# Attention scores laid out with queries on partitions: row maximum as a bias of the exponential, weights turned by transfers or TensorE

## The chip, the cores and the metric

One core of a Trainium2 chip runs the whole program. The core has TensorE (PE), VectorE (DVE), ScalarE (ACT), GpSimd (POOL) and SyncE (SP), which here only issues transfers. The metric is the time of one execution on the device, in microseconds (us); less is better.

## What is computed

The block is `x + attention(layernorm(x)) + ffn(layernorm(x))`, with x of 2 x 1024 tokens x 256. The change touches the attention alone, cut to its core:

```python
q = concat([q_nope, rope(q_rope)])      # 16 heads, 128 + 64 wide
k = concat([k_nope, rope(k_rope)])      # 4 heads, each shared by 4 query heads
attn = einsum('bhqd,bhkd->bhqk', q, k) * scale
attn = where(causal, -inf, attn)        # key > query
attn = softmax(attn, axis=-1)           # minus the row's maximum, exp, over its sum
out  = einsum('bhqk,bhkd->bhqd', attn, vh)
return out.reshape(B, T, H * 128) @ W_o
```

The feed-forward part is an integer-quantised pair of products (1024 inner columns); the change doesn't touch what it computes.

## The kernel before

**Steps.** The attention is a loop of 32 steps n: 4 key heads g, times 8 steps s (2 batches b, 4 query heads r each). A step handles one query head of one batch: 1024 queries by 1024 keys, the lower triangle. Rank 64 latent values stand for keys and values, so that a query or key vector is 128 long (64 latent and 64 rotated), and a value is 64 columns and one of ones (VC = 65), which gives the sum of the weights. Queries, keys and weights are split in a high and a low part, so a product takes three passes: high by high, high by low, low by high.

**Layout of a step.** Scores stand with keys on partitions: j is a tile of 128 keys, and its queries run along the row. `score_chunks` cuts the triangle in 12 chunks of 256 to 512 columns, 4,736 columns in all, into three PSUM banks (`score`, SBANKS = 3). Because the maximum of a query is then a maximum over partitions, the kernel takes it ahead: one to two steps before, `max_unit` forms high by high scores with queries on partitions (4,736 columns again, in `pmax`, two banks), `maxima` (line 863) lets VectorE take each row's maximum with the causal mask, TensorE turns the 8 columns of maxima (L1234), `cast_maxima` (L870, L872) makes two bf16 rows, and SyncE copies them to `m_row`. In `scores`, a product of `ones_b` with `m_row` subtracts the maximum: a fourth pass over each chunk. The names of matmuls in the rows are all at line 1078, the helper `mm`, so they are told apart by their tiles: `m_row,ones_b` is the row of maxima, `k_hi,q_hi` the pass for the maximum, `q_hi,k_hi`, `q_hi,k_lo`, `q_lo,k_hi` the three passes of a score, `kv_tok,p_hi` and `kv_tok,p_lo` the product with the values.

**After the scores.** ScalarE takes the exponential twice, once rounded to f16 (`p_hi`, L684) and once in place (L685); VectorE subtracts (`p_lo`, L996). Both parts are in the layout in which TensorE takes them as weights, and `values` accumulates 36 blocks of 128 x 128, three matmuls each, into the two `head` banks, two key tiles behind the scores.

**Queries.** Three steps ahead TensorE forms the queries of a step (`query`, slots 5 and 6), ScalarE copies them to `q_raw` (L613), GpSimd rotates them in four operations (`rotate`, L469, L472, L475, L478), ScalarE rounds them (`q_hi`, L617, a ring of three), and GpSimd subtracts (`q_lo`, L484).

**Order.** It is written out by hand. A step has 8 slots, one for each key tile; `MISC` and `EXTRA` give the slot of all that shares the one bank `misc`: queries, the turning of normalised heads (`turn`), the output product (`out`), keys of the next head (`ka`, `kb`), the integers of the feed-forward part (`w`, `x`). Each use of the bank waits until the one before is read (`misc_used`). Engines talk by semaphores; every engine works off its own list in order.

## Time and profile before

| | |
|---|---|
| time, median of 3 runs | 780.97 us (780.57 to 782.66) |
| the profiled execution | 779.53 us, of which 777.7 us are its span |
| TensorE busy | 729.5 us (94% of the span) |
| VectorE, ScalarE, GpSimd busy | 580.6, 496.3, 420.4 us |
| first and last pass `q_lo,k_hi` of a score | about 95.8 and 721.9 us after the start |
| four steps in the middle, from 418.3 us on | 18.1, 22.8, 18.2, 17.2 us |

A busy time on TensorE covers each matmul from its start to its modelled end, and matmuls overlap: what one costs in a full stream is the distance to the start of the next. The clock that TensorE was granted stands in the page in tenths, and for a stretch in the windows view, where 1.00 is 2.4 GHz and 0.50 is 1.2 GHz.

### The profile page before, as it was taken

The numbers are of one execution on the slowest core, as the hardware profiler recorded it, in microseconds if no ns is written. First come the engines' busy times: TensorE is split into PE (matmuls) and PEld (weight loads), VectorE is DVE, ScalarE is ACT, GpSimd is POOL, SyncE is SP. The second block draws the span as 40 slices with busy tenths as digits, with TensorE's granted clock in tenths as the row PEclk, the third lists the DMA queues.
The fourth block names the chain that finished last, engine by engine and source line by source line (L and its number), as shares of the span: only waits on it lengthen the run. The fifth ranks groups of instructions, "written<-read, shape, count | busy, mean of one in ns | idle before, by whom it ended". The sixth has DMA issues, their size and how long they took to land.

```text
span 777.7 us, 18089 instructions
## 1 busy us (share of the span) xinstructions
PE 729.5 (94%) x7010; PEld 582.9 (75%) x7084; DVE 580.6 (75%) x1530; ACT 496.3 (64%) x1015; POOL 420.4 (54%) x210
## 2 busy tenths in 40 slices
PE   7996699899999999999999999999999999999856
PEld 5664468688876678878877888788878888887635
DVE  6748478887777777777777768776777787776796
ACT  3555467577556565767577657765776577657754
POOL 4323546666655554676467646764676467620225
PEclk9786699999999999999999999999999999999989
DMA  9754002001300200010001000100000000000003
GB/s 261 256 201 178 1 1 82 16 15 42 124 1 29 82 28 2 21 43 23 2 1 30 1 15 16 42 15 2 1 29 2 1 2 2 2 1 3 14 0 109
DMA packets 20517, 33.08 MB, mean 43 GB/s; under 512 B 2704, under 2 KB 11472, under 8 KB 20304
## 3 DMA queue, kind: packets, MB, share of 16 engines
q1 hardware_dynamic: 19648, 31.34, 12.8%
q8 instruction: 56, 0.92, 0.5%
q10 hardware_dynamic: 784, 0.59, 0.3%
q14 instruction: 29, 0.24, 0.1%
HBM read 21.30 MB, written 10.49 MB: 41 GB/s over the span
## 4 chain that ended last, share of the span: by engine, by line
PE 78%; DVE 10%; issue 4%; ACT 4%; DMA 2%; POOL 1%; SPq 0%; POOLq 0%; ACTq 0%; DVEq 0%
PE psum L1078 74%; PE psum L1275 2%; DMA acc<-in_L_attn_x 2%; DVE hid L1058 1%; DVE small L1027 1%; ACT psum L685 1%; DVE p_lo L996 1%; POOL res L521 1%; ACT p_hi L684 1%; DVE acc L755 1%; PE psum L1101 1%; ACT hid L711 0%; PE psum L1326 0%; DVE kt_a L960 0%; PE psum L1234 0%
## 5 line engine op out<-in xcount | busy, mean ns | idle before, releaser
L684 ACT ACTIVATE p_hi<-psum 128x512 f16<-128x512 f32 (+3 forms) x384 | 187.7, 489 | 169.8 <-PE psum L1078 164.6
L996 DVE TENSOR_TENSOR p_lo<-psum,p_hi 128x512 f16<-128x512 f32 (+3 forms) x384 | 208.4, 553 | 85.7 <-ACT psum L685 84.5
L863 DVE CUSTOM_DVE_ANT_0 junk<-psum,cmask 128x1024 bf16<-128x1024 f32 (+7 forms) x256 | 187.8, 752 | 58.9 <-issue 57.4
L469 POOL TENSOR_TENSOR q_swap<-q_raw,sin_sb 32x1024 f32<-32x1024 f32 x31 | 73.6, 2374 | 228.9 <-ACT q_raw L613 220.5
L685 ACT ACTIVATE psum<-psum 128x512 f32<-128x512 f32 (+3 forms) x384 | 187.2, 487 | 0.0
L1078 PE MATMUL psum<-q_hi,k_hi 128*128 128x512 f32 (+2 forms) x384 | 187.0, 487 | 0.0
L1078 PEld LDWEIGHTS psum<-kv_tok,p_hi 128*128 128x128 f16 x2304 | 116.9, 97 | 53.4 <-issue 38.6
L1078 PE MATMUL psum<-kv_tok,p_hi 128*128 128x65 f16 (+1 forms) x2304 | 151.9, 196 | 0.4 <-DVE p_lo L996 0.4
L1078 PE MATMUL psum<-kv_tok,p_lo 128*128 128x65 f16 x1152 | 138.1, 192 | 0.0
L1078 PE MATMUL psum<-q_hi,k_lo 128*128 128x512 f32 (+2 forms) x384 | 132.1, 344 | 0.0
L1078 PE MATMUL psum<-q_lo,k_hi 128*128 128x512 f32 (+2 forms) x384 | 131.9, 343 | 0.0
L1078 PE MATMUL psum<-k_hi,q_hi 128*128 128x512 f32 (+3 forms) x384 | 106.0, 358 | 11.7 <-DVE small L863 7.7
L1078 PEld LDWEIGHTS psum<-kv_tok,p_lo 128*128 128x128 f16 x1152 | 109.0, 100 | 0.0
L1078 PE MATMUL psum<-m_row,ones_b 128*128 128x384 bf16 (+2 forms) x313 | 100.8, 322 | 1.4 <-DVE p_lo L996 1.4
L1078 PEld LDWEIGHTS psum<-k_hi,q_hi 128*128 128x128 f32 x384 | 65.5, 192 | 32.2 <-DVE small L863 21.3
L484 POOL TENSOR_TENSOR q_lo<-q_raw,q_hi 128x1024 fp32r<-128x1024 f32 x32 | 76.8, 2401 | 15.9 <-PE psum L1078 10.8
L1078 PEld LDWEIGHTS psum<-q_lo,k_hi 128*128 128x128 f32 x384 | 72.7, 189 | 7.3
L1078 PEld LDWEIGHTS psum<-q_hi,k_lo 128*128 128x128 f32 x384 | 73.8, 192 | 4.3
L472 POOL TENSOR_TENSOR q_swap<-q_raw,sin_sb 32x1024 f32<-32x1024 f32 x31 | 74.0, 2388 | 2.4
L475 POOL TENSOR_TENSOR q_raw<-q_raw,cos_sb 64x1024 f32<-64x1024 f32 x31 | 73.9, 2382 | 2.4
L478 POOL TENSOR_TENSOR q_raw<-q_raw,q_swap 64x1024 f32<-64x1024 f32 x31 | 73.6, 2375 | 2.4
L1078 PEld LDWEIGHTS psum<-q_hi,k_hi 128*128 128x128 f32 x384 | 73.9, 193 | 0.0
(172 smaller groups left out, 1205.8 us busy)
## 6 DMA issues: line engine op xcount, KB each, us to landing
wq_split<-w_split SPq DMA_DIRECT2D x4, 1024.0 KB, 5.5
k_rotated<-k_split SPq DMA_DIRECT2D x8, 512.0 KB, 3.7
wq<-wq_split SPq DMA_DIRECT2D x16, 256.0 KB, 2.7
acc<-in_L_attn_x SPq DMA_DIRECT2D x4, 512.0 KB, 7.7
ffn_t<-in_L_attn_W_o SPq DMA_DIRECT2D x1, 2048.0 KB, 20.7
k_hi<-k_rotated SPq DMA_DIRECT2D x8, 256.0 KB, 4.0
k_lo<-k_rotated SPq DMA_DIRECT2D x8, 256.0 KB, 4.5
w_split<-in_L_ffn_w SPq DMA_DIRECT2D x2, 1024.0 KB, 6.0
```

The source lines that it names most:

```text
L469: pool.tensor_tensor(q_swap[0:HR, :], raw[HR:ROPE, :], sin_sb[HR:ROPE, :], ALU.mult)\
L472: pool.tensor_tensor(q_swap[HR:ROPE, :], raw[0:HR, :], sin_sb[0:HR, :], ALU.mult)\
L475: pool.tensor_tensor(raw[0:ROPE, :], raw[0:ROPE, :], cos_sb[0:ROPE, :], ALU.mult)\
L478: pool.tensor_tensor(raw[0:ROPE, :], raw[0:ROPE, :], q_swap[:, :], ALU.add).then_inc(S["pool_step"], 1)
L484: pool.tensor_tensor(q_lo[s % 2][:, :], q_raw[s % 2][:, :], q_hi[n % QRING][:, :], ALU.subtract)\
L521: pool.tensor_tensor(y[:, :, :], y[:, :, :], acc[:, t:t + 2, :], ALU.add).then_inc(S["f_res"], 1)
L684: act.activation(p_hi[j % PRING][:, o:o + used], src, ACT.Exp, scale=SCALE)
L685: act.activation(src, src, ACT.Exp, scale=SCALE).then_inc(S["exp_done"], 1)
L863: ins = dve.tensor_tensor_reduce(junk[:, o:o + w], pmax[:, o:o + w], cmask[:, T - w:T], 1.0, LOWEST, ALU.add, ALU.max, mcol[:, s % 2, i:i ...
L996: dve.tensor_tensor(p_lo[j % PRING][:, o:o + used], score[c % SBANKS][:, w - used:w], p_hi[j % PRING][:, o:o + used], ALU.subtract).then_i ...
L1078: ins = pe.matmul(dst, lhs, rhs, start=start, stop=stop, skip_group_check=True)
L1275: ins = pe.transpose(misc[:, i * P:(i + 1) * P], o_norm[:, 4 * k + i, :], identf[:, :])
```

## The change

Scores now stand with queries on partitions. A step goes over 8 query tiles i in 7 units, in the order 7, 3, 6, 2, 5, (1, 0), 4: the *big* tiles 7, 6, 5, 4 take turns in two places of two PSUM banks each, the *small* ones 3, 2, 1, 0 share one bank.

- The score needs no pass for the maximum. VectorE takes the maximum straight from the scores, negated (`maxima`, L876), and ScalarE adds it as the exponential's bias. The pass of `m_row`, the pass ahead of `max_unit`, `cast_maxima` and the two small transfers of each step are gone. The scale goes into the copy of the queries.
- ScalarE takes each big tile in one operation of 640 to 1024 columns, twice (L676 and the next); a small tile once, in f32, to `p_f32`.
- VectorE subtracts for the big tiles from PSUM (`big_low`, L884, 3,328 columns in 4 operations). For all small tiles together, at the end of a step, it casts 1,280 columns of `p_f32` to f16 (L892) and subtracts (L894), both from SBUF to SBUF (`small_halves`).
- The weights have keys along the row and must be turned. Big tiles: SyncE issues 8 transposing transfers a step, `turn_big`, two for each tile (52 blocks of 128 x 128 in f16, 1.7 MB). Small tiles: in the next step TensorE turns 20 blocks through the bank `misc` in three turns of 8, 8 and 4 (L1283), and ScalarE copies each turn out (L689).
- `values` of tiles 6, 5, 4 and of the small ones come one step later, that of tile 7 at the end of its own step.
- Queries are formed two steps ahead, not three (`q_hi` is a ring of two); GpSimd rotates for the next step.
- `MISC` and `EXTRA` are laid out again over 7 slots.

The diff, cut to its core:

```diff
-CHUNKS = score_chunks()
-MAX_UNITS = [[(7, 0)], [(6, 0)], [(5, 0)], [(4, 0)], [(3, 0), (2, CH)], [(1, 0), (0, CH)]]
+UNITS = ((7,), (3,), (6,), (2,), (5,), (1, 0), (4,))
+BIG = {7: 0, 6: 1, 5: 2, 4: 3}
+SMALL = {3: 0, 2: 1, 0: 2}
+PSRC = 3
+COLS = {7: 0, 5: 0, 6: 2 * CH, 4: 2 * CH + P, 3: 4 * CH, 2: 4 * CH, 1: 4 * CH, 0: 4 * CH + 2 * P}
+PV_AT = {0: (6, 1), 2: (5, 1), 3: (4, 1), 6: (7, 0)}
+PV_SMALL = 4
...
+            def turn_big(n, i, h):
+                q, src = NB * n + BIG[i], slice(0, (i + 1) * P)
+                if n:
+                    sp.wait_ge(S["pv_done"], PV_STEP * (n - 1) + PV_DONE[i])
+                sp.wait_ge(S["lo_done" if h else "hi_done"], q + 1)
+                sp.dma_start(pt_big[i][:, h * (i + 1):(h + 1) * (i + 1), :], p_src[q % PSRC][:, h, src], transpose=True)\
+                  .then_inc(p_in[q % PSRC], 16)
...
-            rotate(2, 2, 6)
             for n in range(LAST):
+                if n + 1 < LAST:
+                    rotate(n + 1, n + 1, misc_index(n - 1, "query", 1) + 1 if n else 4)
...
-                if n + 3 < LAST:
-                    rotate(n + 3, n + 3, misc_index(n, "query", 1) + 1)
-                if n + 2 < LAST:
-                    pool.wait_ge(S["score_done"], NC * (n + 1))
-                    query_low(n + 2, n + 2)
+                if n + 1 < LAST:
+                    query_low(n + 1, n + 1)
...
-                            act.activation(p_hi[j % PRING][:, o:o + used], src, ACT.Exp, scale=SCALE)
-                            act.activation(src, src, ACT.Exp, scale=SCALE).then_inc(S["exp_done"], 1)
+                        act.activation(p_src[q % PSRC][:, 0, 0:w], src, ACT.Exp, bias=nb).then_inc(S["hi_done"], 1)
+                        act.activation(src, src, ACT.Exp, bias=nb).then_inc(S["exp_done"], 1)
+                    else:
+                        if n:
+                            act.wait_ge(S["small_lo"], n)
+                        ins = act.activation(p_f32[:, OFF[i]:OFF[i] + w], src, ACT.Exp, bias=nb)
...
+            def maxima(n, u):
+                dve.wait_ge(S["score_done"], NS * n + u + 1)
+                for i in UNITS[u]:
+                    dve.tensor_reduce(sm["mcol"][:, NT * (n % 2) + i:NT * (n % 2) + i + 1],
+                                      psum[:, COLS[i]:COLS[i] + (i + 1) * P], AX.X, ALU.max, negate=True)\
+                       .then_inc(S["max_done"], 1)
...
+            def small_halves(n):
+                dve.wait_ge(S["small_free"], len(SMALL) * (n + 1))
+                if n:
+                    dve.wait_ge(S["misc_full"], misc_index(n, "pt", 2) + 1)
+                dve.tensor_copy(p_small[:, 0, :], p_f32[:, :]).then_inc(S["small_hi"], 1)
+                dve.wait_ge(S["small_hi"], n + 1)
+                dve.tensor_tensor(p_small[:, 1, :], p_f32[:, :], p_small[:, 0, :], ALU.subtract).then_inc(S["small_lo"], 1)
...
-                mm(o, ones_b[:, 0:P], m_row[s % 2][:, qs], not diagonal, False)
-                mm(o, k_hi[b][:, ks], qh[:, qs], False, False)
-                mm(o, k_lo[b][:, ks], qh[:, qs], False, False)
-                mm(o, k_hi[b][:, ks], ql[:, qs], False, True, S["score_done"])
+                        mm(o, qh[:, qs], k_hi[b][:, ks], not diagonal, False)
+                        mm(o, qh[:, qs], k_lo[b][:, ks], False, False)
+                        ins = mm(o, ql[:, qs], k_hi[b][:, ks], False, True)
...
+            def turn_small(m, k, idx):
+                pe.wait_ge(S["small_lo"], m + 1)
+                pe.wait_ge(S["misc_used"], idx)
+                for t, (h, i, j) in enumerate(TURNS_B[k]):
+                    o = OFF[i] + j * P
+                    ins = pe.transpose(misc.bitcast(F16)[:, t * P:(t + 1) * P], p_small[:, h, o:o + P], ident16[:, :])
+                ins.then_inc(S["misc_full"], 1)
```

Three places show what the order has become. On VectorE, at the end of a step and the beginning of the next, before (the maxima of later steps between the subtractions of this one):

```order
L996 TENSOR_TENSOR p_lo0<-psum,p_hi0 128x512 [waits pv_done,exp_done]
L996 TENSOR_TENSOR p_lo0<-psum,p_hi0 128x512 [waits exp_done]
L860 MEMSET small 128x1 [waits max_done]
L863 ISA junk,small<-psum,cmask 128x640
L863 ISA small 128x1
L996 TENSOR_TENSOR p_lo1<-psum,p_hi1 128x512 [waits pv_done,exp_done]
L888 RECIPROCAL small<-psum 128x4 [waits pv_done]
L892 TENSOR_TENSOR o_norm<-psum,small 128x4x64 [waits norm_step]
```

and now (the last two operations of a step are L892 and L894; the row behind them is the maximum of the next step's tile 7):

```order
L884 TENSOR_TENSOR p_src1<-psum,p_src1 128x768 [waits exp_done]
L876 TENSOR_REDUCE small<-psum 128x1 [waits score_done]
L911 TENSOR_TENSOR o_lo1<-psum,o_hi1 128x512 [waits o_hi_done]
L892 CAST p_small<-p_f32 128x1280 [waits misc_full,small_free]
L894 TENSOR_TENSOR p_small<-p_f32,p_small 128x1280 [waits small_hi]
L876 TENSOR_REDUCE small<-psum 128x1 [waits score_done]
L884 TENSOR_TENSOR p_src2<-psum,p_src2 128x640 [waits exp_done]
L876 TENSOR_REDUCE small<-psum 128x1 [waits score_done] x2
L884 TENSOR_TENSOR p_src0<-psum,p_src0 128x1024 [waits exp_done]
```

Every maximum now stands between the scores of its own tile and that tile's exponential, and the two operations on the small tiles come behind the maximum of tile 4, the last of the step. On TensorE, in the first slots of a step, before:

```order
L1078 MATMUL psum<-k_hi1,q_hi0 128x512 [waits max_read]
L1078 MATMUL psum<-k_hi1,q_hi0 128x256
L1078 MATMUL psum<-m_row0,ones_b 128x512 [waits lo_done]
L1078 MATMUL psum<-q_hi2,k_hi1 128x512
L1078 MATMUL psum<-q_hi2,k_lo1 128x512
L1078 MATMUL psum<-q_lo0,k_hi1 128x512
L1078 MATMUL psum<-kv_tok,p_hi2 128x65 [waits lo_done]
```

and now, behind the scores of tile 7 and the values of tile 6 (the last row is that of those values):

```order
L1084 MATMUL psum<-kv_tok,pt_big6 128x65
L1283 MATMUL psum<-ident16,p_small 128x128 [waits misc_used,small_lo]
L1283 MATMUL psum<-ident16,p_small 128x128 x7
L1084 MATMUL psum<-cmask,ident 128x128 [waits small_free]
L1084 MATMUL psum<-k_hi0,q_hi1 128x512
L1084 MATMUL psum<-k_lo0,q_hi1 128x512
L1084 MATMUL psum<-k_hi0,q_lo1 128x512
L1283 MATMUL psum<-ident16,p_small 128x128 [waits misc_used,small_lo]
L1283 MATMUL psum<-ident16,p_small 128x128 x7
L1084 MATMUL psum<-k_hi0,q_hi1 128x512 [waits lo_done]
```

The passes with `m_row` and with `max_read` are gone, and the turns of the small tiles stand there, the first behind `small_lo`, which L894 gives. On GpSimd a step is these five rows in either kernel; now:

```order
L468 TENSOR_TENSOR q_swap<-q_raw1,sin_sb 32x1024 [waits misc_used,qlo_done]
L471 TENSOR_TENSOR q_swap<-q_raw1,sin_sb 32x1024 [waits pool_step]
L474 TENSOR_TENSOR q_raw1<-q_raw1,cos_sb 64x1024 [waits pool_step]
L477 TENSOR_TENSOR q_raw1<-q_raw1,q_swap 64x1024 [waits pool_step]
L483 TENSOR_TENSOR q_lo1<-q_raw1,q_hi1 128x1024 [waits pool_step,qhi_done]
```

The first waits for the second half of the queries, which now leaves `misc` in slot 5 of 7 of a step; the fifth no longer waits for `score_done`.

## Rows read from the trace of the kernel before

**Rows 1.** The page: busy time by engine, and TensorE's granted clock in tenths

```profile
PE 729.5 (94%) x7010; PEld 582.9 (75%) x7084; DVE 580.6 (75%) x1530; ACT 496.3 (64%) x1015; POOL 420.4 (54%) x210
PEclk9786699999999999999999999999999999999989
```

**Rows 2.** Windows of four steps, 418.3 to 494.6 us: their sums and means

```profile
sum 76.30, PE 76.30 PEld 62.85 DVE 57.94 ACT 51.42 POOL 47.56; mean PE 19.07 PEld 15.71 DVE 14.49 ACT 12.85 POOL 11.89
```

**Rows 3.** The page: the chain that ended last, share by engine

```profile
PE 78%; DVE 10%; issue 4%; ACT 4%; DMA 2%; POOL 1%; SPq 0%; POOLq 0%; ACTq 0%; DVEq 0%
```

**Rows 4.** Timeline of PE at 404 us: start, duration, line, tiles, size

```profile
404.08 0.39 PE L1078 MATMUL psum<-qc_lo,wq 128*128 128x512 f32 x1
404.31 0.39 PE L1078 MATMUL psum<-qc_hi,wq 128*128 128x512 f32 x1
```

**Rows 5.** Timeline of PE, 145.9 to 149.1 us; in brackets the idle time ahead

```profile
145.90 0.22 PE L1078 MATMUL psum<-kv_tok,p_hi 128*128 128x65 f16 x2
...
145.99 0.22 PE L1078 MATMUL psum<-ident,cmask 128*128 128x128 bf16 x1
146.04 0.33 PE L1078 MATMUL psum<-m_row,ones_b 128*128 128x384 bf16 x1
146.07 0.47 PE L1078 MATMUL psum<-q_hi,k_hi 128*128 128x384 f32 x1
146.38 0.33 PE L1078 MATMUL psum<-q_hi,k_lo 128*128 128x384 f32 x1
146.55 0.34 PE L1078 MATMUL psum<-q_lo,k_hi 128*128 128x384 f32 x1
149.00 0.51 PE L1078 MATMUL psum<-k_hi,q_hi 128*128 128x256 f32 x2 [2.11 <-DVE small L863]
```

**Rows 6.** Groups of instructions by form: count, busy us, mean ns, idle before

```profile
L996 DVE TENSOR_TENSOR p_lo<-psum,p_hi 128x512 f16<-128x512 f32 x160 | 110.2, 689 | 65.4 <-ACT psum L685 65.4
L996 DVE TENSOR_TENSOR p_lo<-psum,p_hi 128x384 f16<-128x384 f32 x96 | 53.1, 553 | 17.7 <-ACT psum L685 16.9 <-DVE m_cast L872 0.4
L1027 DVE TENSOR_REDUCE small<-hid 128x1 f32<-128x1024 f32 x16 | 18.7, 1213 | 2.5 <-ACT hid L711 2.5
L684 ACT ACTIVATE p_hi<-psum 128x512 f16<-128x512 f32 x160 | 95.4, 596 | 120.3 <-PE psum L1078 118.6
L631 ACT ACTIVATE ffn_t<-psum 128x1024 bf16<-128x1024 bf16 x2 | 2.1, 1030 | 0.0
```

**Rows 7.** Timeline of DVE's operations from SBUF to SBUF, and POOL's beside them

```profile
144.99 2.86 DVE L966 TENSOR_SCALAR acc<-acc,small 128x1024 f32<-128x1024 f32 x1
144.94 2.36 POOL L478 TENSOR_TENSOR q_raw<-q_raw,q_swap 64x1024 f32<-64x1024 f32 x1
147.53 2.53 POOL L484 TENSOR_TENSOR q_lo<-q_raw,q_hi 128x1024 fp32r<-128x1024 f32 x1 [0.24 <-POOL q_raw L478]
152.98 0.74 DVE L966 TENSOR_SCALAR acc<-acc,small 128x1024 f32<-128x1024 f32 x1
231.72 0.97 DVE L960 TENSOR_TENSOR kt_a<-kt_a,kt_b 128x512 f32<-128x512 f32 x1
229.75 2.38 POOL L478 TENSOR_TENSOR q_raw<-q_raw,q_swap 64x1024 f32<-64x1024 f32 x1
259.87 0.69 DVE L960 TENSOR_TENSOR kt_a<-kt_a,kt_b 128x512 f32<-128x512 f32 x1
```

**Rows 8.** Windows around the wait at 146.9 us: busy time, then granted clock (PEclk)

```profile
146.80:150.20 3.40, 1.29 (x16) 1.01 (x15) 3.40 (x9) 0.87 (x2) 3.03 (x2) 1.00 0.00 0
150.30:153.60 3.30, 2.98 (x20) 2.61 (x21) 2.76 (x10) 1.25 (x3) 0.00 (x0) 0.50 0.02 5
```

**Rows 9.** Transfers: count, KB each, us from issue to landing; SP's own time

```profile
k_rotated<-k_split SPq DMA_DIRECT2D x8, 512.0 KB, 3.7
wq<-wq_split SPq DMA_DIRECT2D x16, 256.0 KB, 2.7
k_lo<-k_rotated SPq DMA_DIRECT2D x8, 256.0 KB, 4.5
L368 SPq DMA_DIRECT2D m_row<-m_cast x64: 620/633/1130, 90.8 to 707.4; - x64
```

575 lines of the change are left out of this document (265 added, 310 removed).

## The prediction

> **What bounds the kernel now.** I read the page first: TensorE is busy for 94% of the span, and its clock stands at the full level from the fourth slice nearly to the end [rows 1]. The chain of work that ended last is TensorE's for 78%, with no other engine over 10% [rows 3]. The windows of four steps settle it: 76.3 us, in all of which TensorE is busy, while VectorE has 14.49 us of work in a mean step of 19.07, ScalarE 12.85 and GpSimd 11.89 [rows 2]. So a step costs what TensorE's stream costs, and nothing waits. The question for the change is how much it takes out of that stream, and whether the stream stays unbroken.
>
> **What leaves and enters TensorE's stream.** A matmul costs the distance to the start of the next. A pass over 512 columns costs 0.23 us [rows 4], so the pass for the maximum, 4,736 columns, costs 4,736 / 512 x 0.23 = 2.1 us a step. For the row of maxima, `m_row` and the first pass of a 384-column chunk take from 146.04 to 146.38, 0.34 us together, and the next pass alone 0.17 [rows 5]; so the row costs 0.17 for 384 columns, 2.1 us for 4,736. Removed: 4.2 us. Added: 20 turns of 128 x 128 in f16, at the price of the 128-wide bf16 matmul ahead of `m_row`, 0.05 us (145.99 to 146.04) [rows 5]: 1.1 us with their weight loads. The three passes of a score and the 36 blocks of values (0.09 us each, 145.90 to 145.99 [rows 5]) stay. TensorE's work falls by 3.1 us, from 19.07 to 16.0 us a step.
>
> **The other engines.** ScalarE: two widths, 596 ns for 512 columns and 1,030 for 1,024, give 0.85 ns a column and 0.16 us fixed [rows 6]. Twelve operations and 1,280 columns fewer save 3.0 us, and the copies of the turns (1.03, 1.03, 0.6) add 2.7: even, and far from a bound. VectorE: 689 and 553 ns for 512 and 384 columns give 1.06 ns a column and 0.15 fixed [rows 6]; eight subtractions and 1,280 columns fewer save 2.5 us, and the two operations on the small tiles add 2.4 (below). The maximum costs what a reduction of 1,024 columns does, 1.2 us, about as now. VectorE stays at some 14 us, under 16. GpSimd's five operations stay. None of these becomes the bound by its sum of work.
>
> **The new wait.** The bound comes from an order of events at each step's end. The last scores of a step are those of tile 4. Only then does VectorE take their maximum (640 columns, 0.82 us), and behind it, in its list, it casts the small tiles' 1,280 columns and subtracts. TensorE can't turn the small tiles before `small_lo`, and its own work in between is short: values of tile 7 (8 x 0.09 = 0.7), scores of tile 7 (six passes of 0.23 and a mask, 1.4), values of tile 6 (0.6), in all 2.8 us. Everything of the next step is queued behind this turn on TensorE, and on ScalarE the copy of the turn stands ahead of the exponentials of tile 7, so no engine can run past it.
>
> How long do the two operations take? The like of the cast, from SBUF to SBUF, took 0.74 us for 1,024 columns with GpSimd idle, and the like of the subtraction 0.69 for 512 [rows 7]. With 256 and 768 more columns (0.53 and 1.04 ns each) that is 0.88 and 1.49 us. But the same instructions took 2.86 and 0.97 us with GpSimd at work [rows 7]: the first started at 144.99, 0.05 us behind GpSimd's L478, and ended at 147.85, 0.55 us after L478's end at 147.30; the second started at 231.72 and ended 0.56 us after L478's end at 232.13. Both stood still until GpSimd's instruction was over, and GpSimd's next one, started at 147.53, took 2.53 in place of 2.38: it stood still for VectorE's rest. In the new order GpSimd is at work there for certain: the queries leave `misc` in slot 5 of 7, and from then on four operations of 2.38 us follow each other. The cast can wait for up to 2.38 us, and the subtraction, which has to wait for the cast, finds GpSimd's next operation in possession: up to 2.38 again. Bounds: 0 and 4.8 us. I take 3.0, the second wait nearly in full and the first in part (the cast may come first, where the queries were late).
>
> The Trainium skill (SBUF — State Buffer, Who interferes with whom) says the same more sharply: a cast in a two-port mode, or an operation with two SBUF inputs, and a GpSimd operation exclude each other for a whole instruction, and the one that issues second waits. By that rule alone, with both in full, the sum would hold 4.8 in place of 3.0 us, some 55 us more in all; by a mere sharing of bandwidth (0.97 to 0.69 as a ratio of 1.4) it would hold 1.0 in place of 3.0.
>
> Sum, from the end of the last scores: 0.8 (maximum) + 0.6 (what VectorE still has ahead of it: the subtraction of tile 5 or the low half of a turned head) + 0.9 + 1.5 + 0.1 (two semaphores) = 3.9; less 2.8 of cover, 1.1; plus 3.0 of standing still: TensorE waits **4.1 us a step**. Before, the list on TensorE had no wait for an operation of its own step's end.
>
> **Smaller waits.** The three turns share `misc`. The second must wait for ScalarE's copy of the first, 1.03 us and two semaphores, under a cover of 0.7 (scores of tile 3): 0.5. The third waits behind two exponentials of 1,024 columns (1 us each): 0.5. The small bank's next scores: 0.3. Turned heads now wait for a normalisation of the same slot, in two steps of four: 0.5 on average. Sum 1.8 us, between 0 and 3.
>
> **Transfers.** 1.7 MB a step are turned by 8 transfers. SyncE spends 0.63 us on a small one [rows 9], 5 us a step, within its time. Moving: no row shows a turning transfer. From 2.7 us for 256 KB to 3.7 for 512 KB [rows 9] is 1 us for 256 KB, 6.6 us a step. The latency, 2 to 4.5 us, has cover: a tile's values come four or five slots of some 3 us later. The upper bound takes each 256 KB as a transfer by itself, 4.5 us as `k_lo` [rows 9]: 6.5 x 4.5 = 29 us a step, more than a step has. I take the lower, as the transfers may overlap.
>
> The Trainium skill prices it twice: 261 GB/s for turning transfers (DMA: Bandwidth & Descriptors, Latency and other measured facts), by which a step's take 6.6 us, and 1,309 ns for a block of 128 x 128 (VectorE: DVE Perf Modes, The three transpose paths); as a rate that would be 52 x 1.3 = 68 us a step and a kernel of over 2,200 us.
>
> **The clock.** A wait of 2.11 us left 1.29 us of work in a window of 3.4 us [rows 5, 8]; in the next window the granted clock was 0.50, that is 1.2 GHz, and then it rose again. A wait of 4.1 us in each step should bring the same in each. At half the clock 3.4 us of stream lose 1.7 us; bounds 0 and 1.7 a step. I take 0.7, since part of that stretch waits for ScalarE anyhow.
>
> **Sum.** A step: 16.0 + 4.1 + 1.8 = 21.9 us, and 0.7 for the clock, 22.6, against 19.07: +3.5. For 31 steps with a step behind them that is +109. Ahead of the loop the passes for the first maxima and two small transfers fall away, behind it the last step's turns and values stand uncovered: some 10 us each, which I set against each other. 777.7 + 109 = 787 + 100, that is 887 us of span; with the 1.8 us around it 889, and the median stands 1.4 above the profiled execution: **about 888 us**.
>
> **Rivals.**
> 1. *GpSimd is out of the way*, so that the small tiles' operations need 2.4 us, and VectorE has nothing ahead of them. The wait falls to 0.5, a step to 16.0 + 0.5 + 1.8 = 18.3, the clock holds: 31 x -0.8 = -25, **about 756 us**. It decides from the length of the wait: with the smaller waits at 1.8, everything under 1.3 us is faster than before. For it speaks only that GpSimd works 11.89 of 19 us [rows 2]; against it, that these are the same microseconds. Its limit, no waits at all, is 31 x -3.1 = -96, 685 us. Chance 0.08.
> 2. *The transfers don't keep up.* At 29 us a step instead of 19: 31 x 10 = +310, **about 1,090 us**. TensorE would then wait for `p_in` and ScalarE for a free `p_src` (three buffers). Chance 0.09.
> 3. The forecast, new wait with GpSimd's part: 0.83. Its own range: half the blocking and no fall of the clock, 16.0 + 2.6 + 1.8 = 20.4, +41, 820 us; full blocking and 1.2 for the clock, 16.0 + 5.9 + 1.8 + 1.2 = 24.9, +180, 960 us.
>
> **Range and chances.** The forecast's own range, cut to 945 at the top, where full blocking in each of 31 steps is unlikely, and let down to 800 at the bottom for a blocking of a third, holds all but 2 in 10 of the chance: 800 to 945 us. This kernel's runs can tell a difference of about 0.3%. Faster: most of rival 1, 0.06. Same: 0.03. Slower: 0.91.
>
> **What the new profile would show.** The removal: TensorE's groups of `m_row` and of the pass for the maximum gone, its work without waits near 16 us a step. The wait: among the waits, TensorE's turns of `p_small` held by VectorE's L894, some 31 times, 3 to 5 us each. The blocking: L892 with a mean near 2 us and not 0.9, L894 near 3.5 and not 1.5, each ending a fixed time after an operation of GpSimd's. The clock: half the level behind each wait. The transfers: landing within 2 to 5 us, and nobody waiting for `p_in`. I am wrong in the mechanism if L892 and L894 together take under 3 us, and in the sign if TensorE's wait for them is under 1.3 us a step.

## The result, and the profile after

The changed kernel takes **930.73 us** (median of three runs, 925.66 to 933.94) against 780.97 before: a ratio of 1.190, 95% interval 1.181 to 1.199. The forecast was 888 us, range 800 to 945. The side, the mechanism and the range held; the time is 43 us over the forecast.

The page of the changed kernel, its busy times and the granted clock, and its chain by engine, answer [rows 1] and [rows 3]:

```profile
PE 732.6 (79%) x6919; PEld 570.3 (61%) x6922; DVE 651.1 (70%) x826; ACT 527.8 (57%) x727; POOL 462.7 (50%) x210
...
PEclk9666898899987898779989998988988998989898
...
PE 44%; DVE 30%; ACT 17%; issue 6%; DMA 2%; POOL 1%; POOLq 0%; ACTq 0%; SPq 0%
```

TensorE has gone from 94% of the span to 79%, and the chain that was TensorE's for 78% is now TensorE's for 44% and VectorE's for 30%. The clock, which before stood at 9 from the fourth slice on, dips all through the loop.

Four steps in the middle, from one cast of the queries to the fifth, answer [rows 2]. A row has start and end, length, then busy time and number of instructions of PE, PEld, DVE, ACT and POOL, and the granted clock:

```profile
515.67:538.05 22.38, 17.58 (x197) 14.11 (x195) 15.54 (x18) 14.35 (x22) 13.42 (x5) 0.92 0.44 75
538.05:562.80 24.75, 20.68 (x219) 17.22 (x218) 16.77 (x22) 13.27 (x20) 13.44 (x5) 0.93 0.39 77
562.80:588.36 25.56, 20.17 (x204) 16.03 (x203) 18.98 (x25) 14.43 (x21) 13.39 (x5) 0.87 0.39 78
588.36:608.63 20.27, 16.30 (x182) 12.61 (x181) 15.97 (x19) 13.03 (x19) 13.40 (x5) 0.92 0.64 120
sum 92.96, PE 74.73 PEld 59.97 DVE 67.27 ACT 55.07 POOL 53.65; mean PE 18.68 PEld 14.99 DVE 16.82 ACT 13.77 POOL 13.41
```

A mean step is 23.24 us long and holds 18.68 of TensorE's work; before, both were 19.07. So 4.6 us of each step are waits of TensorE.

Which waits, is in the list of waits (engine, its instruction, what released it: us in total, times, longest):

```profile
PE psum L1283 <- DVE p_small L894: 94.8, 32, 4.5
...
PE psum L1291 <- ACT q_raw L609: 17.4, 14, 1.9
...
PE psum L1084 <- ACT pt_small L689: 15.9, 17, 1.1
...
PE psum L1283 <- ACT pt_small L689: 5.0, 12, 1.2
```

The first is the wait of the prediction: the first turn of the small tiles behind VectorE's subtraction, 3.0 us a step on average, in every step. SBUF is the memory in which the program's own tiles lie (`p_f32`, `p_small`, `q_raw`), PSUM the one that the matmuls write. Why the subtraction comes so late is in the groups (count, busy us, mean ns), to be held against [rows 7]:

```profile
L894 DVE TENSOR_TENSOR p_small<-p_f,p_small 128x1280 f16<-128x1280 f32 x32 | 108.7, 3396 | 1.1
...
L474 POOL TENSOR_TENSOR q_raw<-q_raw,cos_sb 64x1024 f32<-64x1024 f32 x31 | 92.6, 2986 | 2.4
L471 POOL TENSOR_TENSOR q_swap<-q_raw,sin_sb 32x1024 f32<-32x1024 f32 x31 | 88.9, 2866 | 2.4
...
L892 DVE CAST p_small<-p_f 128x1280 f16<-128x1280 f32 x32 | 49.0, 1530 | 2.2 <-ACT p_f L681 2.2
```

and, for one step's end, in the timelines of VectorE, GpSimd and TensorE, one fence for each (start, duration):

```profile
543.80 0.94 DVE L892 CAST p_small<-p_f 128x1280 f16<-128x1280 f32 x1
544.77 3.52 DVE L894 TENSOR_TENSOR p_small<-p_f,p_small 128x1280 f16<-128x1280 f32 x1
```

```profile
541.66 2.39 POOL L468 TENSOR_TENSOR q_swap<-q_raw,sin_sb 32x1024 f32<-32x1024 f32 x1
544.13 2.81 POOL L471 TENSOR_TENSOR q_swap<-q_raw,sin_sb 32x1024 f32<-32x1024 f32 x1
547.02 3.49 POOL L474 TENSOR_TENSOR q_raw<-q_raw,cos_sb 64x1024 f32<-64x1024 f32 x1
```

```profile
544.51 0.82 PE L1084 MATMUL psum<-kv_tok,pt_big 128*128 128x65 f16 x21
548.35 0.62 PE L1283 MATMUL psum<-ident,p_small 128*128 128x128 f16 x8 [3.01 <-DVE p_small L894]
```

The subtraction started at 544.77, 0.64 us behind the start of GpSimd's L471. It ended at 548.29, 1.35 us after that operation's end at 546.94, and an undisturbed one takes 1.49 (below). So it stood still for about 2 us. The same distances, within 0.02 us, stand in the 30 steps in which GpSimd is at work there; in the last two steps, without it, the subtraction took 1.49. GpSimd pays as well: L471 began at 544.13, while the cast was still running (it ended at 544.74), and took 2.81 in place of 2.38; L474 began at 547.02, while the subtraction was running, and took 3.49.

The clock around the longest of the waits (4.5 us, 571.0 to 575.5) answers [rows 8]; after the bracketed counts stands the granted clock:

```profile
568.50:571.90 3.40, 2.42 (x28) 1.69 (x28) 3.38 (x3) 2.04 (x3) 3.24 (x3) 1.00 0.48 95
571.90:575.30 3.40, 0.00 (x0) 0.00 (x0) 3.39 (x1) 0.00 (x0) 3.32 (x2) 0.74 0.06 11
575.30:578.70 3.40, 3.21 (x21) 2.60 (x21) 2.64 (x4) 2.14 (x3) 2.34 (x1) 0.50 0.03 7
578.70:582.00 3.30, 3.30 (x34) 2.52 (x33) 0.99 (x2) 2.54 (x4) 0.00 (x0) 0.75 0.92 192
```

With the wait the clock falls to 0.50, and what follows (3.21 us busy of 3.40) runs at it. Over the whole span 245 us lie at half the clock, against 59 before.

The turning transfers, the answer to [rows 9]: SyncE's time for an issue (least, median, most, ns), and the median time to landing:

```profile
L369 SPq DMA_TRANSPOSE pt_big<-p_src x256: 1199/1232/3807, 91.8 to 868.3; - x128
```

```profile
pt_big<-p_src SPq DMA_TRANSPOSE x256, 3.1
```

TensorE waited for them three times, 2.8 us in all.

Outside of the steps: the first low by high pass of a score (`k_hi,q_lo`, before `q_lo,k_hi`) starts at 87.0 us (95.8 before), and behind the last one, at 862.1, there are 66.8 us (55.8 before): -9 and +11, which nearly cancel.

### The profile page after: what moved, and what is told of

Its sections match the earlier page's. It is cut to its first block, busy times and chain, and to the rows that moved or that the text cites. A ratio compares the mean times of both kernels' runs of the same rounds, so it can differ in the third digit from the quotient of the medians.

```text
span 928.9 us, 17035 instructions
## 1 busy us (share of the span) xinstructions
PE 732.6 (79%) x6919; PEld 570.3 (61%) x6922; DVE 651.1 (70%) x826; ACT 527.8 (57%) x727; POOL 462.7 (50%) x210
## 4 chain that ended last, share of the span: by engine, by line
PE 44%; DVE 30%; ACT 17%; issue 6%; DMA 2%; POOL 1%; POOLq 0%; ACTq 0%; SPq 0%
PE psum L1084 36%; DVE p_small L894 12%; PE psum L1283 6%; DVE p_small L892 5%; ACT p_src L676 4%; ACT pt_small L689 4%; DVE small L876 3%; ACT psum L677 3%; DVE p_src L884 3%; ACT q_raw L609 2%; DVE o_lo L911 1%; ACT q_hi L614 1%; DMA pt_big<-p_src 1%; PE psum L1291 1%; ACT o_hi L664 1%
## 5 line engine op out<-in xcount | busy, mean ns | idle before, releaser
L876 DVE TENSOR_REDUCE small<-psum 128x1 f32<-128x1024 f32 (+7 forms) x256 | 189.5, 751 | 117.8 <-PE psum L1084 117.6
L483 POOL TENSOR_TENSOR q_lo<-q_raw,q_hi 128x1024 fp32r<-128x1024 f32 x32 | 75.8, 2369 | 316.2 <-ACT q_hi L614 316.2
L689 ACT ACTIVATE pt_small<-psum 128x1024 f16<-128x1024 f16 (+1 forms) x96 | 84.9, 884 | 201.6 <-PE psum L1283 201.5
L1084 PE MATMUL psum<-k_hi,q_hi 128*128 128x512 f32 (+2 forms) x384 | 179.1, 466 | 24.9 <-POOL q_lo L483 13.5
L676 ACT ACTIVATE p_src<-psum,small 128x1024 f16<-128x1024 f32 (+3 forms) x128 | 121.8, 951 | 52.9 <-DVE small L876 51.1
L1283 PE MATMUL psum<-ident,p_small 128*128 128x128 f16 x640 | 71.8, 273 | 99.9 <-DVE p_small L894 94.8
L1084 PE MATMUL psum<-k_lo,q_hi 128*128 128x512 f32 (+2 forms) x384 | 145.6, 379 | 0.0
L1084 PE MATMUL psum<-k_hi,q_lo 128*128 128x512 f32 (+2 forms) x384 | 145.1, 378 | 0.0
L884 DVE TENSOR_TENSOR p_src<-psum,p_src 128x1024 f16<-128x1024 f32 (+3 forms) x128 | 129.9, 1014 | 15.5 <-ACT psum L677 15.2
L1283 PEld LDWEIGHTS psum<-ident,p_small 128*128 128x128 f16 x640 | 52.1, 124 | 119.8 <-DVE p_small L894 98.7
L677 ACT ACTIVATE psum<-psum,small 128x1024 f32<-128x1024 f32 (+3 forms) x128 | 118.5, 926 | 0.0
L894 DVE TENSOR_TENSOR p_small<-p_f,p_small 128x1280 f16<-128x1280 f32 x32 | 108.7, 3396 | 1.1
L1084 PE MATMUL psum<-kv_tok,pt_big 128*128 128x65 f16 (+1 forms) x2496 | 103.2, 197 | 2.8 <-DMA pt_big<-p_src 2.8
L1084 PEld LDWEIGHTS psum<-kv_tok,pt_big 128*128 128x128 f16 x2496 | 87.9, 100 | 25.1 <-issue 20.8
L474 POOL TENSOR_TENSOR q_raw<-q_raw,cos_sb 64x1024 f32<-64x1024 f32 x31 | 92.6, 2986 | 2.4
L471 POOL TENSOR_TENSOR q_swap<-q_raw,sin_sb 32x1024 f32<-32x1024 f32 x31 | 88.9, 2866 | 2.4
L477 POOL TENSOR_TENSOR q_raw<-q_raw,q_swap 64x1024 f32<-64x1024 f32 x31 | 82.0, 2646 | 2.4
```

The lines of the kernel that those rows point to most:

```text
L471: pool.tensor_tensor(q_swap[HR:ROPE, :], raw[0:HR, :], sin_sb[0:HR, :], ALU.mult)\
L474: pool.tensor_tensor(raw[0:ROPE, :], raw[0:ROPE, :], cos_sb[0:ROPE, :], ALU.mult)\
L477: pool.tensor_tensor(raw[0:ROPE, :], raw[0:ROPE, :], q_swap[:, :], ALU.add).then_inc(S["pool_step"], 1)
L676: act.activation(p_src[q % PSRC][:, 0, 0:w], src, ACT.Exp, bias=nb).then_inc(S["hi_done"], 1)
L677: act.activation(src, src, ACT.Exp, bias=nb).then_inc(S["exp_done"], 1)
L689: act.activation(pt_small[:, 8 * k:8 * k + m, :], misc.bitcast(F16)[:, 0:m * P].rearrange("p (t q) -> p t q", q=P), ACT.Copy)\
```

## The experiments

All are edits of the changed kernel. Each was timed beside the kernel before (780 to 782 us); ratios are to that.

**1. GpSimd out of the way.**

```diff
             for n in range(LAST):
+                if n:
+                    pool.wait_ge(S["small_lo"], n)
                 if n + 1 < LAST:
...
```

> Edit: GpSimd starts the rotation of the next step's queries only after VectorE has finished both operations on the small tiles of the step before; the two operations, their order and all of VectorE's other work stay. Theory A (GpSimd's operation stops VectorE's): in the changed kernel the cast took 1.53 us on average and the subtraction 3.40, and the last two steps, without GpSimd, showed 0.82 and 1.49. So they should fall to about 0.82 and 1.49, 2.6 us a step, TensorE's wait at the first turn from 3.0 to under 1 us a step; 31 x 2.6 = 80 us from 930.7 gives 850, and if the clock then stays up as well, down to 800. Theory B (the slow pair comes from the transposing transfers' use of SBUF, or is simply late in VectorE's list): the two operations stay near 1.5 and 3.4 us and the time near 925 to 935. Theory C (the wait moves to the low half of the queries, which GpSimd now makes later): the pair gets short, but TensorE waits for q_lo by some 2 us a step and the time stays over 880.

Measured: **825.5 us**, ratio 1.055 (1.052 to 1.058). The two groups, the mean of four steps, and the wait that is left:

```profile
L896 DVE TENSOR_TENSOR p_small<-p_f,p_small 128x1280 f16<-128x1280 f32 x32 | 47.8, 1492 | 1.1
L894 DVE CAST p_small<-p_f 128x1280 f16<-128x1280 f32 x32 | 35.6, 1111 | 1.3 <-ACT p_f L683 1.0
```

```profile
sum 80.23, PE 69.16 PEld 55.39 DVE 57.42 ACT 55.21 POOL 47.40; mean PE 17.29 PEld 13.85 DVE 14.36 ACT 13.80 POOL 11.85
```

```profile
PE psum L1285 <- DVE p_small L896: 23.6, 23, 1.2
```

Not one operation was taken away, and 105 us are gone. The subtraction is at 1.49 us in all 32 steps, the cast at 0.82 in 24 of them and near 2.0 in the other eight, mostly every fourth, where it meets GpSimd's low half of the queries (L483). Theory A holds: 825.5 lies between its 850, for the waits alone, and its 800, with the clock back up. The granted clock in these four steps is 1.00. A step went from 23.24 to 20.06: TensorE's busy time from 18.68 to 17.29 and its waits from 4.6 to 2.8, so that 1.4 of the 3.2 us came from the clock. At the first turn the wait fell by 2.3 us a step in these steps, from 3.1 to 0.8; TensorE's other waits rose by 0.5.

**2. No operation from SBUF to SBUF: the small tiles from PSUM.** ScalarE takes the exponential of a small tile twice; VectorE subtracts in three operations.

```diff
-                        ins = act.activation(p_f32[:, OFF[i]:OFF[i] + w], src, ACT.Exp, bias=nb)
+                        act.activation(p_small[n % 2][:, 0, OFF[i]:OFF[i] + w], src, ACT.Exp, bias=nb)
+                        ins = act.activation(src, src, ACT.Exp, bias=nb)
...
-                dve.tensor_copy(p_small[:, 0, :], p_f32[:, :]).then_inc(S["small_hi"], 1)
...
-                dve.tensor_tensor(p_small[:, 1, :], p_f32[:, :], p_small[:, 0, :], ALU.subtract).then_inc(S["small_lo"], 1)
...
+                dve.tensor_tensor(p_small[n % 2][:, 1, OFF[i]:OFF[i] + w], psum[:, COLS[i]:COLS[i] + w],
+                                  p_small[n % 2][:, 0, OFF[i]:OFF[i] + w], ALU.subtract).then_inc(S["small_lo"], 1)
```

> Edit: the two SBUF to SBUF operations are gone. ScalarE takes each small tile's exponential twice, as for the big tiles (high half in f16 to a ring of two, then in place), and VectorE subtracts for a small tile from PSUM, in three operations of 512, 384 and 384 columns spread over the step; the first turn needs the high halves alone. GpSimd's order is unchanged. Theory A (what costs is the pair of operations that GpSimd can stop, and its place behind the step's last maximum): TensorE's wait at the first turn, 3.0 us a step, nearly vanishes, VectorE's subtractions take 0.55 to 0.7 us as the like ones do; ScalarE gets 1280 columns and 4 operations more, 1.7 us a step, within its time. 31 x 3.0 = 93 us and the clock's share back: 790 to 840 us. Theory B (the extra time lies in transfers or in ScalarE's copies of the turns): little changes, or ScalarE's extra 1.7 us a step shows, 900 to 960.

Measured: **840.8 us**, ratio 1.075 (1.068 to 1.082). VectorE's group of 512 columns, GpSimd's L473, and what TensorE waits for now:

```profile
L473 POOL TENSOR_TENSOR q_raw<-q_raw,cos_sb 64x1024 f32<-64x1024 f32 x31 | 73.2, 2362 | 2.4
...
L889 DVE TENSOR_TENSOR p_small<-psum,p_small 128x512 f16<-128x512 f32 x32 | 22.0, 688 | 18.4 <-ACT psum L679 18.4
```

```profile
PE psum L1082 <- DVE p_small L889: 43.4, 41, 2.1
```

GpSimd works beside VectorE as in the changed kernel, and neither stops the other: a subtraction from PSUM takes 0.69 us, GpSimd's operations 2.36. TensorE no longer waits for VectorE at the turns. That is theory A, just past the slow end of its range (790 to 840). A new wait came in: the bank of the small tiles is free for the next scores only when VectorE has subtracted, 43.4 us in all. That this wait, and not ScalarE's further work, keeps the run at the slow end was not tried.

**3. The transfers left out.**

```diff
+                if n == 0:
                     sp.dma_start(pt_big[i][:, h * (i + 1):(h + 1) * (i + 1), :], p_src[q % PSRC][:, h, src], transpose=True)\
                       .then_inc(p_in[q % PSRC], 16)
+                else:
+                    sp.sem_inc(p_in[q % PSRC], 16)
```

> Edit: the transposing transfers are issued in step 0 alone; in all later steps SyncE only counts the semaphore up, so big tiles are multiplied with step 0's turned weights (the output is then not the block's; the transfers' moving is what is left out, all waits stay in place). Theory A (blocking by GpSimd, transfers hidden): TensorE waited for turned weights for 2.8 us in all, so the time falls by 0 to 10 us, 920 to 931, and the subtraction on the small tiles stays at 3.4 us. Theory B (the transfers cost: they slow SBUF accesses of VectorE and GpSimd, or hold a weights' buffer): the subtraction falls towards 1.5 us, GpSimd's operations from 2.6 to 3.0 us back to 2.4, and the time to 850 or less.

Measured: **928.6 us** (924.2 to 931.3), no difference from 930.7. The subtraction on the small tiles stays as it was:

```profile
L897 DVE TENSOR_TENSOR p_small<-p_f,p_small 128x1280 f16<-128x1280 f32 x32 | 108.7, 3398 | 1.1
```

1.7 MB of turning transfers a step cost nothing here, neither by waits nor by slowing another engine (GpSimd's four rotations take 2.49, 2.88, 3.01 and 2.62 us on average, and 2.49, 2.87, 2.99 and 2.65 with the transfers). Rival 2 is out.

**4 and 6. The clock alone: 14 and 24 filling products ahead of the wait.**

```diff
+                pe.wait_ge(S["misc_used"], idx)
+                if k == 0:
+                    keep_clock(misc, 14)
                 pe.wait_ge(S["small_lo"], m + 1)
-                pe.wait_ge(S["misc_used"], idx)
```

> Edit: ahead of its wait for the small tiles' low half TensorE does 14 bf16 products of 256 columns into the bank that it is about to write (at 0.11 us each about 1.5 us at full clock), which nobody reads; all else stays. It measures what the clock costs. Theory A1 (the idle of 3 to 4.5 us in each step lets the granted clock fall, and the fall costs time): the time at half the clock falls from 245 us to under 130, and the kernel from 930.7 to 870 to 900 us, since a stretch of 3.4 to 7 us at half the clock holds 2 to 4 us of work that would take half of that. Theory A2 (the fall lies where TensorE waits anyway): the time at half the clock falls but the kernel stays within 925 to 935. If the filling is too short for the clock, the stretches stay at 245 us and the run says nothing on the price; if it is too long, it delays the turn and adds up to 31 x 1.5 = 47 us.

> Edit: as in the run with 14 filling products, with 24 of them (2.6 us at full clock at 0.11 each). With 14 the time at half the clock fell from 245 to 139 us and the kernel from 930.7 to 908.0. Theory A1 (what the clock's fall costs is in proportion to the time at half the clock, 23 us for 105): with a clock that falls nearly only ahead of the loop and behind it, some 60 to 100 us at half, the price falls by another 10 to 15 us, less what the filling delays: where it outlasts the wait (1.8 us in the shortest steps, 3.3 to 4.4 in the others) 0 to 0.8 us in one step of four, 0 to 6 us in all: 893 to 905 us. Theory A2 (14 already took all there was to take): 908 to 925, since the filling delays the turns.

Measured: **908.0 us** with 14 (906.5 to 909.5) and **894.5** with 24 (894.0 to 904.5). The time at half the clock is 245 us without filling, 139 with 14, 70 with 24. The granted clock of both, 14 first:

```profile
PEclk7776999899997999699999999999999999999988
```

```profile
PEclk9667999999999999999999999999999999999988
```

Each microsecond less at half the clock gave back 0.21 us, both times (22.7 for 106, 36.2 for 175). The subtraction stays at 3.40 us in both. So of the changed kernel's loss some 36 to 39 us (the 186 us that it has more at half the clock, times 0.21) are the clock's, by an edit that leaves the late data where they were. It is rather more than that: with 24 the filling outlasts the subtraction by about 0.9 us in every fourth step, so that the edit costs something too.

**5. VectorE's order: the two operations ahead of the last maximum** (slot j = 6).

```diff
+                            small_halves(n)
                         maxima(n, j)
...
-                    if n < LAST and j == 6:
-                        small_halves(n)
```

> Edit: VectorE does the two operations on the small tiles ahead of the maximum of the step's last tile (4) and no longer behind it; GpSimd's order stays. It tests the term of the prediction that puts 0.8 us of the wait down to that maximum and 0.6 to what else stands ahead. Theory A (the operations are stopped by GpSimd wherever they stand): they still take 1.5 to 2 and 3.4 us, TensorE's first turn gets its data up to 0.8 us earlier, but the maximum, and with it the exponentials of tile 4, come 3 to 5 us later, so that the wait reappears at ScalarE and in TensorE's next big tiles: 925 to 950 us. Theory B (the place in VectorE's list is the cost): the wait of 3.0 us falls by 0.8 to 1.4, and 25 to 45 us go: 885 to 905.

Measured: **937.1 us** (935.2 to 938.3). The subtraction, ScalarE's wait for the maximum, and TensorE's waits at the turns:

```profile
L894 DVE TENSOR_TENSOR p_small<-p_f,p_small 128x1280 f16<-128x1280 f32 x32 | 109.2, 3413 | 1.1
```

```profile
ACT p_src L676 <- DVE small L876: 219.4, 65, 7.0
...
PE psum L1282 <- DVE o_lo L911: 58.4, 15, 4.6
...
PE psum L1282 <- DVE p_small L894: 15.8, 9, 1.8
...
PE psum L1282 <- DVE acc L917: 14.2, 7, 2.2
```

Theory A. GpSimd stops the two operations there as well, and another place in the list only makes something else late. TensorE's wait for the subtraction fell from 94.8 to 15.8 us, but at the same turns it now waits 58.4 and 14.2 us for L911 and L917, the two operations by which VectorE frees the shared bank and which stand behind the pair now: 88.4 us together, so that next to nothing was won there. ScalarE's wait for the maxima rose from 51 to 219 us.

**7. As 1, and the high halves by ScalarE**, so that VectorE's cast is gone.

```diff
+                        act.activation(p_small[:, 0, OFF[i]:OFF[i] + w], src, ACT.Exp, bias=nb)
                         ins = act.activation(p_f32[:, OFF[i]:OFF[i] + w], src, ACT.Exp, bias=nb)
...
-                dve.tensor_copy(p_small[:, 0, :], p_f32[:, :]).then_inc(S["small_hi"], 1)
...
-                pe.wait_ge(S["small_lo"], m + 1)
+                if k == 0:
+                    pe.wait_ge(S["small_free"], len(SMALL) * (m + 1))
+                else:
+                    pe.wait_ge(S["small_lo"], m + 1)
```

> Edit: GpSimd starts behind the small tiles' operation, as in the first experiment (825.5 us), and besides ScalarE writes the high halves of the small tiles itself (a second exponential of each, f16), so that VectorE's cast is gone, the first turn waits for no VectorE operation at the step's end, and the subtraction alone is left there. Theory A (what is left of the wait, 23.6 us at small_lo in that run, and its share of the clock, comes from the 0.82 us cast and the 1.49 us subtraction behind the last maximum): 825 less 15 to 25 gives 800 to 810 us. Theory B (ScalarE, 528 of 822 us busy, is by now what the turns wait for; 1.7 us a step more on it): the gain is eaten, 820 to 840, as in the run that took all small tiles from PSUM (840.8).

Measured: **807.8 us**, ratio 1.034 (1.029 to 1.039), theory A. ScalarE's 1.7 us more a step (578 us busy in all) cost less than the cast at the step's end had.

**8 to 11. A version that beats both.** High halves by ScalarE; low halves of tiles 3 and 2 from SBUF in mid-step, where GpSimd waits for the queries; those of tiles 1 and 0 from PSUM. Besides three placings: the queries' cast in slot 2, tile 6's values in slot 1, turns of 8, 7 and 5 blocks. In the diff `small_low` takes the step, its first tile, its blocks of 128 columns, its last tile, and whether the source is PSUM.

```diff
-PV_AT = {0: (6, 1), 2: (5, 1), 3: (4, 1), 6: (7, 0)}
+PV_AT = {1: (6, 1), 2: (5, 1), 3: (4, 1), 6: (7, 0)}
...
-QHI_SLOT = 4
+QHI_SLOT = 2
...
+                        if j == 3:
+                            small_low(n, 3, 4, 3, False)
+                        if j == 5:
+                            small_low(n, 2, 3, 2, False)
                         maxima(n, j)
...
+                        if j == 6:
+                            small_low(n, 1, 3, 0, True)
```

> Edit: the version that the traces point to. ScalarE writes the high halves of the small tiles; VectorE subtracts tile 3 and tile 2 from f32 in SBUF in the middle of the step (512 and 384 columns, ahead of the maxima of slots 3 and 5), when GpSimd in the changed kernel has nothing to do (it waited 316 us for the cast of the queries), and tiles 1 and 0 from PSUM, where GpSimd can't stop it, at the step's end. Besides: the cast of the queries in slot 2, the first two turns of the step further apart from the values (tile 6's values a slot later), turns of 8, 7 and 5 blocks. Theory A (with both causes of the wait gone, blocking and order, TensorE's stream of some 16 to 17 us a step shows): no wait for the small tiles over 0.5 us, a step of 18.0 to 19.0 us, 755 to 790 us in all. Theory B (the shared bank for turns, queries and heads, and ScalarE with 18 us of work a step, are the bound at 20 us): 800 to 825.

> Edit: of the best version (773.6 us) only what has nothing to do with the small tiles' halves: the cast of the queries in slot 2, tile 6's values in slot 1, turns of 8, 7 and 5 blocks. VectorE's cast and subtraction stay at the step's end. Theory A (the best version's gain comes from the halves made elsewhere and earlier): the subtraction stays near 3.4 us and TensorE's wait at 3 us a step or longer, since tile 6's values no longer stand between the first scores and the turn, so 0.6 us of cover is lost: 925 to 955 us. Theory B (the placing of the other work gives a good part of the gain by itself): 890 us or less.

> Edit: of the best version only the small tiles' halves: high halves by ScalarE; low halves of tiles 3 and 2 by VectorE from SBUF in mid-step, of tiles 1 and 0 from PSUM at the end. The queries' cast, the values and the turns stay as in the changed kernel. Theory A (the wait for the small tiles was the cost): 930.7 less 110 to 130 us; with what is left of ScalarE's copies and late queries, 800 to 820 us, better than the run that kept a subtraction from SBUF at the end (807.8) by 0 to 10, and the subtractions in mid-step mostly at 0.55 to 0.7 us. Theory B (ScalarE is the bound): as the run with all from PSUM, 835 to 845.

> Edit: the best version (773.6 us) with the turns of the small tiles put ahead of the values of the same slot in TensorE's list, the values of tiles 6, 5, 4 in slots 0, 1, 2 and those of the small ones in slot 3. What is left in its trace are waits of TensorE of 0.6 us for the small bank behind the last turn and of 0.8 to 1.2 for the shared bank, some 7 us in four steps. Theory A: the values now cover ScalarE's copies of the turns, 0.2 to 0.3 us a step, 763 to 772 us. Theory B (SyncE's transfers now come too late for values a slot earlier, or the stream is as full as it gets): 772 to 780.

Measured, in the order of the expectations: halves and placings together (8) **773.6 us** (ratio 0.990, 0.985 to 0.994); the placings alone (9) 944.5 (940.6 to 946.5); the halves alone (10) 808.4 (806.1 to 815.9); and (11) both with the turns ahead of the values and the values a slot earlier, **761.2 us**, ratio 0.975 (0.972 to 0.978).

Theory A holds in 8, 9 and 10; 11 came out 2 us under the range of its theory A. The placings alone cost 14 us: TensorE's wait for the subtraction grew to 138.8 us, as tile 6's values no longer covered it (first fence). The same placings on top of the new halves gave 35: TensorE's waits for ScalarE's copies of the turns, for the shared bank ahead of the turned heads and for the low half of the queries were 19.9, 17.8 and 12.9 us with the halves alone (second fence), and 5.9, 11.2 and none with both:

```profile
PE psum L1284 <- DVE p_small L895: 138.8, 32, 7.0
```

```profile
PE psum L1291 <- ACT pt_small L690: 19.9, 49, 2.4
...
PE psum L1299 <- ACT q_raw L609: 17.8, 14, 1.7
PE psum L1090 <- POOL q_lo L483: 12.9, 9, 1.9
```

A miss: with the halves alone I expected the subtractions in mid-step mostly undisturbed. That of tile 2 was (0.55 us), that of tile 3 took 0.89 on average instead of 0.68, since in 12 steps it met GpSimd's last rotation (L477). And the run was not faster than run 7. Mid-step is not free of GpSimd with the queries' cast in slot 2 either: in run 8 tile 2's subtraction took 0.94 us on average, since in half of the steps it met the low half of the queries (L484). The last version, its busy times, clock and four steps:

```profile
PE 665.0 (88%) x6922; PEld 521.3 (69%) x6922; DVE 554.0 (73%) x858; ACT 578.0 (76%) x855; POOL 417.6 (55%) x210
...
PEclk9786599999999999999999999999999999998989
```

```profile
sum 74.31, PE 68.75 PEld 55.36 DVE 54.52 ACT 61.55 POOL 47.55; mean PE 17.19 PEld 13.84 DVE 13.63 ACT 15.39 POOL 11.89
```

A step of 18.58 us with 17.19 of TensorE's work; 19.07 before. So scores with queries on partitions do pay, by 2.5%. Taking what GpSimd can stop from between the last scores and the first turn is needed for it and is not enough: by itself (runs 7 and 10) it left the kernel 3.4 and 3.8% slower than before, and only together with the placings is it faster. The last version's gain of 12 us over 773.6 lies mostly in the first half of the loop (10 us over its 16 steps), where keys and integers share the bank. Nearly 8 of them are shorter waits of TensorE for ScalarE's copies of the turns ahead of the keys' and integers' products (9.4 us in place of 17.1).

## Why the prediction was right, and where it was off

Steady steps first: forecast 22.6 us, measured 23.24 over four steps, each term against its own measurement. The terms as written add up to 890 us and not 888 (889 and 1.4), a slip that changes nothing.

- **TensorE's work: 16.0 forecast, 17.3 measured** (the granted clock at 1.00 in run 1; 17.2 in the last version). The step that failed here is the price of the row of maxima. I read 0.34 us for `m_row` and the first pass together [rows 5], took off 0.17, the price of the pass after, and put 2.1 us a step on `m_row`. Summing the distance from each matmul to the start of the next over the four steps of [rows 2] and over the four of run 1, the first pass of a chunk costs 0.25 us and the second 0.18 even without `m_row`: 0.07 of what I gave to the row belong to the first pass itself. Before, the mask, `m_row` and the first pass cost 4.65 us a step together; in run 1 the mask and the first pass cost 3.32. So the row was worth 1.3 us and not 2.1. The pass for the maximum was 2.3 (forecast 2.1), the turns 1.25 (forecast 1.1), and the values rose from 3.4 to 3.7, the queries from 2.4 to 2.5, the turned heads and the output product from 1.8 to 2.0, which I had left unchanged. Net -1.8, not -3.1.
- **The new wait: 4.1 forecast, 3.1 measured** in those steps (3.16, 3.01, 4.47 and 1.81), 3.0 over all; every fourth step it is 1.8 and not 3 to 5. The blocking was as said: L894 3.40 us (forecast 3.5) and L892 1.53 (forecast near 2), together 2.6 over what they take undisturbed (forecast 3.0). What was mis-sized is the cover. From the end of the last scores to the end of the subtraction the four steps took 7.3 us (forecast 6.9: the pair 5.0 and not 5.5, what stands ahead of it 2.3 and not 1.4). Of that time TensorE's other work and waits covered 4.2 us and not 2.8, with the clock up (run 1) as with it down. I had left out three things, one of which stands there in each of the four steps: the turned heads (0.8 us, twice), the output product (1.5) and a wait of 1.8 for GpSimd's low half of the queries, which is why the wait of that fourth step is the shortest. Both halves of the cause are shown: with GpSimd moved (run 1) or PSUM as source (run 2) it is gone; without the transfers (run 3) or in another order (run 5) it stays. The Trainium skill (SBUF — State Buffer, Who interferes with whom) has the rule: an operation with two SBUF inputs, or a cast in a two-port mode, and one of GpSimd's exclude each other; the trace agrees, with 4.93 us for the pair beside GpSimd's operations and 2.31 without.
- **Smaller waits: 1.8 forecast, 1.5 measured** (TensorE's idle time of 4.6 in the four steps less the 3.1). The sum held by luck. The second and third turn, forecast at 1.0, waited 0.2, and the small bank, forecast at 0.3, next to nothing; the turned heads waited 0.55 (forecast 0.5), but for ScalarE's copy of the queries and not for a normalisation; and 0.45 are that wait for the low half of the queries (1.8 in one step of four), for which the sum had no term.
- **The clock: 0.7 forecast, 1.3 to 1.4 measured**, by two roads: 18.68 of busy time against 17.29 with the clock at 1.00, and 0.21 x 186 / 31 = 1.3 from the filling runs. I had 0.7 for 3.4 us at half the clock, 0.21 a microsecond, and that price is the one that the filling runs gave. The length was short: 186 / 31 = 6.0 us of a step are at half the clock that were not before (in these four steps it is 4.3, at 0.33 of TensorE's busy time a microsecond).
- **Errors that cancel.** +1.3, -1.0, -0.3, +0.6: the step came out at +0.6, and that it came so near is luck in part. Over 31 steps that is 20 us of the 43 that were missing.
- **The early steps** hold the rest. From the first low by high pass to the last it is 775.1 us against 626.0, +149; 31 times the steady +4.2 gives 129. In the first half of the loop, where keys and integers take further turns in the shared bank, steps were 22 to 32 us long in the changed kernel, and mostly 19 to 24 before. I had taken four steady steps for all 31, and that is where the remaining 20 us lie. The trace names two waits of TensorE that stand in the first half alone: 11.1 us ahead of the keys' products and 6.4 ahead of the integers', both for ScalarE's copy of a turn (L689) out of the shared bank. Run 8 has both still (10.8 and 6.3), run 11 half of them (4.9 and 4.5).
- **Prologue and tail** (-10 and +10 forecast): -9 and +11.
- **Transfers:** landing in 3.1 us at the median (forecast 2 to 5), next to nobody waiting (2.8 us in all). An issue takes SyncE 1.23 us and not 0.63: eight are 10 us a step and still hidden. The upper bound, 29 us a step, is refuted by the last version's steps of 18.6 us with all transfers in them. So is the reading of the Trainium skill (VectorE: DVE Perf Modes, The three transpose paths) by which 1,309 ns for a block would be a rate. My lower price, 6.6 us a step, is under what the trace shows: the queue's packets took 46.0% of the span of the 16 DMA engines, and 11.6% in run 3, which is 10.3 us a step for the transfers. The Trainium skill's 261 GB/s for turning transfers (DMA: Bandwidth & Descriptors, Latency and other measured facts) gives 6.6 us as well, an estimate. Whether they could go faster if somebody waited for them, no run tells.
- **The other engines.** ScalarE's work, which I had as even, rose from 12.85 to 13.8 us a step (run 1); I had counted 1,280 columns fewer for it and for VectorE, and it is 1,536 and 1,408. VectorE's stayed at 14.4 without the blocking. Neither became the bound.
- **Rival 1** (GpSimd out of the way) had 756 us. Run 1 makes its first condition true (the pair takes 2.6 us, 2.4 in the rival), not the second, that VectorE has nothing ahead of it, and gives 825. Of the 69 us between them TensorE's work is again the most (1.3 us a step, 40 us); waits of 2.8 us a step where the rival had 2.3 are 15, and the rest is the early steps.

## What to carry to other kernels

When an operation on the critical path of VectorE reads and writes SBUF alone, look at what GpSimd does at that moment before you price it: here 2.3 us of work became 4.9, and one wait in GpSimd's list gave back 105 us. Another place in the list did not help, because something else then stood behind the stopped operations. A wait of TensorE costs more than its own length when the granted clock falls with it; a run with filling products in the wait tells how much. And before you price a matmul that goes by what it and its neighbour take together, look for a place where the neighbour stands alone: here the first pass of a score cost 0.25 us and not the 0.18 of the second.

## What I had not expected of the hardware

- The stop goes both ways: GpSimd's operations of 2.37 us took 2.87 (L471) and 2.99 us (L474) on average, since they stand still for VectorE's; beside subtractions from PSUM they stayed at 2.36 to 2.38.
- The subtraction took 3.51 to 3.56 us in every step but the last two, however long the cast ahead of it took (0.81 to 3.01 us). In all 30 steps an operation of GpSimd's had begun 0.64 to 0.66 us before the subtraction, while the cast was running, and ended 2.16 to 2.20 us after the subtraction's start. The cast thus seems to bring the two into step: what follows it meets an operation of GpSimd's that has hardly begun, and stands still for 2.0 of its 2.4 us.
- 1.7 MB of turning transfers in a step, of 160 to 256 KB each, land 3.1 us after their issue at the median (9.3 at the most), and leaving them out changed neither the time nor any other engine's durations.
- Cheap products that nobody reads made the kernel 36 us faster (24 in each step), with 97 us of TensorE's busy time in them and in those of the prologue.
